# One block of value weighing moved ahead of the output projection on TensorE, in an attention and expert layer over eight batch elements

## The reference, cut to what matters

```python
h = _layernorm(x) * (1 + ca) + sa
x = x + ga * attn(h)                     # (8, 256, 128)
h = _layernorm(x) * (1 + cb) + sb
x = x + gb * experts(h)

# attn: 16 heads of 8, keys within 32 tokens of the query
Q, K, V = split(h @ W_qkv.T)
scores = where(mask, Q @ K.T / sqrt(8), -inf)
out = softmax(scores) @ V                # "the values weighed"
attn = out @ W_o.T                       # "the output projection"
```

## Time and profile before

| | us |
|---|---|
| median of three runs | 168.95 |
| their range | 168.29 to 169.29 |
| the profiled execution | 168.28 |
| its span | 166.5 |
| TensorE busy in it (matmuls) | 147.6 |
| VectorE busy | 129.4 |
| ScalarE busy | 88.6 |
| GpSimd busy | 54.9 |
| mean DMA traffic | 37 GB/s |

### The profile page before, as it was taken

How to read it: one execution, slowest core, us unless ns; L and a number is a source line. 1 busy time by engine, 2 the same in 40 slices (tenths; PEclk the granted TensorE clock), 3 DMA queues, 4 the chain that set the end, 5 groups by cost and what they waited for, 6 DMA issues and landing times.

```text
span 166.5 us, 5054 instructions
## 1 busy us (share of the span) xinstructions
PE 147.6 (89%) x1966; PEld 124.2 (75%) x1968; DVE 129.4 (78%) x353; ACT 88.6 (53%) x173; POOL 54.9 (33%) x109
## 2 busy tenths in 40 slices
PE   6799986979899989999899989998999899966943
PEld 2478875868689968997699869985998599644833
DVE  3456457698989998889899989997989888763572
ACT  3143765356838473855477456845672555535220
POOL 6422130140063605370526143523412252163030
PEclk9999999999999999999999999999999999998799
DMA  5864241102330242013401330044003400100002
GB/s 143 234 191 28 24 41 12 34 1 35 22 47 0 32 32 69 6 31 20 78 4 16 35 48 4 4 46 52 0 4 41 57 0 4 33 0 0 0 0 63
DMA packets 47430, 6.21 MB, mean 37 GB/s; under 512 B 42416, under 2 KB 47024, under 8 KB 47408
## 3 DMA queue, kind: packets, MB, share of 16 engines
q1 hardware_dynamic: 47264, 5.90, 22.6%
q10 hardware_dynamic: 144, 0.00, 0.0%
HBM read 3.81 MB, written 2.10 MB: 35 GB/s over the span
## 4 chain that ended last, share of the span: by engine, by line
PE 58%; DVE 23%; issue 9%; ACT 7%; POOL 2%; POOLq 0%; ACTq 0%; DVEq 0%
PE ps L637 8%; PE ps L669 8%; PE ps L729 7%; DVE blkmax L936 5%; PE ps L597 3%; PE ps L652 3%; PE ps L722 3%; PE ps L787 3%; PE ps L756 3%; PE ps L707 3%; DVE shift L954 2%; PE ps L709 2%; PE ps L708 2%; PE ps L611 2%; PE ps L615 2%
## 5 line engine op out<-in xcount | busy, mean ns | idle before, releaser
L352 POOL TENSOR_TENSOR act_w<-act,cw 128x512 f32<-128x512 f32 x15 | 15.7, 1044 | 49.1 <-issue 33.5
L936 DVE TRANSPOSE_TENSOR_REDUCE blkmax<-ps 128x44 f32<-128x1408 f32 x16 | 26.3, 1642 | 4.9 <-PE ps L644 4.9
L486 ACT ACTIVATE probs<-ps 128x704 f32<-128x704 f32 x32 | 23.2, 754 | 6.8 <-PE ps L652 6.0
L669 PE MATMUL ps<-probs,v_bd 128*36 128x64 f32 (+2 forms) x640 | 23.3, 227 | 0.5 <-ACT probs L486 0.5
L669 PEld LDWEIGHTS ps<-probs,v_bd 128*36 128x36 f32 x640 | 20.9, 114 | 3.0 <-issue 0.9
L637 PEld LDWEIGHTS ps<-q_sb,k_bd 32*128 32x128 f32 x640 | 19.4, 186 | 4.7 <-issue 3.4
L637 PE MATMUL ps<-q_sb,k_bd 32*128 32x96 f32 (+2 forms) x640 | 21.3, 274 | 0.6 <-ACT probs L486 0.3
L493 ACT ACTIVATE o_t<-ps 36x512 f32<-36x512 f32 x16 | 9.5, 593 | 15.8 <-PE ps L669 15.7
L499 ACT ACTIVATE tanh_g<-ps 128x512 f32<-128x512 f32 x16 | 9.6, 597 | 15.4 <-PE ps L709 15.4
L729 PE MATMUL ps<-wd_sb,act_t 128*128 128x128 f32 x128 | 16.7, 276 | 0.7 <-ACT act_t L503 0.7
L729 PEld LDWEIGHTS ps<-wd_sb,act_t 128*128 128x128 f32 x128 | 15.9, 191 | 1.0 <-ACT act_t L503 0.9
(11 more groups left out here) (102 smaller groups left out, 281.5 us busy)
## 6 DMA issues: line engine op xcount, KB each, us to landing
x_sb<-x SPq DMA_DIRECT2D x8, 128.0 KB, 2.5
v_spill<-v_sb SPq DMA_DIRECT2D x8, 128.0 KB, 2.3
v_bd<-v_spill SPq DMA_DIRECT2D x32, 32.0 KB, 2.8
out<-out_sb SPq DMA_DIRECT2D x7, 128.0 KB, 2.4
wgu_sb<-w_gu SPq DMA_DIRECT2D x1, 512.0 KB, 4.3
wm_sb<-wmod SPq DMA_DIRECT2D x1, 256.0 KB, 3.8
wd_sb<-w_down SPq DMA_DIRECT2D x1, 256.0 KB, 5.4
con<-consts SPq DMA_DIRECT2D x1, 244.0 KB, 2.9
```

Of the source, the lines that this page charges most:

```text
L352: nc.gpsimd.tensor_tensor(act_w[:, t, :].rearrange("p (e i) -> p e i", e=E), act[:, t, :].rearrange("p (e i) -> p e i", e=E), view(cw[:, t ...
L486: nc.scalar.activation(probs[:, t, hgs, cols], ps[:, hgs, cols], ACT.Exp, scale=float(DH) ** -0.5).then_inc(probs_ready, 1)
L669: last = nc.tensor.matmul(ps[p0:p0 + VW, OB, c0 + lo * KB:c0 + (hi + 1) * KB], v_bd[:, i % VB, kb, hg, :], view(probs[:, t, hg, at:at + 1] ...
L936: nc.vector.tensor_reduce(blkmax[:, t, :, live(t):live(t) + LIVE], view(ps[:, 0, live(t) * KB:live(t) * KB + 1], [[BANK, NHG], [KB, LIVE], ...
```

## The change

In the steady steps on TensorE, `weigh_values(i, 0, 0)` is issued between the transposes of the normalised attention output and the output projection, and no longer behind the second scores. Everything else stays in its place, and all waits are as they were.

```diff
                 subtract_max(i, 0, 0)
                 subtract_max(i, 0, 1)
                 transpose_on(i - 1)
+                weigh_values(i, 0, 0)
                 output_projection(i - 1)
                 up(i - 2, 1)
                 scores(i, 1)
-                weigh_values(i, 0, 0)
                 weigh_values(i, 0, 1)
                 transpose_x1(i - 1)
                 transpose_act(i - 2, 0)
```

## The result

| | before | changed |
|---|---|---|
| median of four runs | 169.01 | 182.78 |
| their range | 168.29 to 169.29 | 180.41 to 184.42 |
| profiled execution | 168.28 | 183.99 |
| its span | 166.5 | 182.2 |

The change makes the kernel slower. The ratio is 1.0708, with an interval from 1.0647 to 1.077; it is taken from those two of the four executions (181.57 and 180.41) in which TensorE's clock was held back less, and the profiled one is not among them. The same kernel, measured again later beside runs of before at 169.23, took 186.10 (185.85 to 186.30), a ratio of 1.099, from 1.0967 to 1.1014. That spread is itself part of the answer.

A forecast was written before the change was run, and what follows sets the result against it. The end was set by a lane changing between TensorE and VectorE, with the stretch hanging on the output projection's start. Profiled 168.28 + 11.4 wait - 0.3 regained = 179.4; against the median 180.05, forecast 180.0 us, range 175.5 to 185.5.

The forecast's parts named there:

- the first rival: Moved block on TensorE: values already in place, only 0.12 us lost per step, 169.6 us; chance 0.08.
- the sum: Output projection's delays in steps 2 to 7, from the values' landings plus release and block: 11.4 us in all.
- The block and the gap: Before the output projection: a 0.69 us block in a 0.47 us idle makes the projection 0.12 us late per step.
- The size of the wait: TensorE waiting for four value transfers: projection late by 2.84, 1.59, 2.05, 2.39, 1.35 and 1.15 us, 11.4 in all.
- My bounds: Output projection's total delay: 7.2 us with shortest landings and a usual spill in step 2, 16.0 with the longest.
- What comes back: Behind the projection, at the second layer norm and shifts: 0.05 us regained per step, 0.3 in all.
- The idle ahead of L597: TensorE idle ahead of the second layer norm's transposes: about 0.5 us, released by ScalarE's xn.
- The clock: TensorE's granted clock falling in the new idles: 185.1 us for three of six steps, 190.2 for all; chance 0.12.
- my own price: Cost of a granted-clock fall where TensorE is the bound: 1.7 us, read from the fall at 152 to 156.
- the two cases: Full wait at full clock, 180.0 us, chance 0.76; and the clock falling in three of six steps, 185.1 us.
- the range: Forecast time from 175.5 to 185.5 us, covering the wait's bounds and clock falls in up to three steps.
- The second rival's condition: Placed values early and TensorE's lane setting the step behind the projection: 0.57 us gained per step, 165.5 us; chance 0.04.

The follow-up runs named there:

- the idle matmuls: Four idle matmuls of 512 columns added to the changed kernel, between the transposes and the moved block: 183.06 us, ratio 1.0852.
- the two kernels with the wait alone: Order of before, with the wait for the four value transfers put ahead of the output projection: 184.59 us; with four idle matmuls ahead of that wait: 178.54 us.
- the run of the old values: Changed order with a third v_bd buffer, weighing the previous element's values in the steady steps, so no wait for its own: 170.29 us, ratio 1.0108.
- the kernel with two transfers on ScalarE: Changed kernel with the last two of the four placed-value transfers issued by ScalarE instead of SyncE in steps 3 to 7: 178.55 us, ratio 1.0539.
- one transfer on ScalarE: Changed kernel with the last of the four placed-value transfers issued by ScalarE instead of SyncE in steps 3 to 7: 179.73 us, ratio 1.0585.

## Why the prediction was right, and where it was not

- **What decides.** Right. The block's wait for its own values holds the projection. Taking the wait away left 1.6 us over the 168.74 of before on that chip (the first rival's side, though it gave 0.7), putting the wait there alone gave the projections' delays of the sum (7.5 against 7.3), and with one issue fewer on SyncE the wait shrank by 0.6 us a step.
- **The block and the gap.** The block starts 0.36 us behind L749 and takes 0.75, not 0.69; a block measured inside a pair is a little short. The move without the wait makes the projection 0.19 late and a step 0.12 to 0.15 longer (steps 3 to 6), where I had 0.12.
- **The size of the wait.** 11.0 against 11.4. The terms that rested on how long the four issues take differ both ways (step 5: 1.84 against 2.39), and the sum was 11.0 and 12.2 in the two profiles of the changed kernel and 13.9 with the idle matmuls. My bounds from 7.2 to 16.0 hold them all.
- **What comes back.** Right: 0.04 and 0.03 in the two steps that can be read so (3 and 6), where I took off 0.05. The idle ahead of L597 is 0.54, as said.
- **The clock.** Here the step failed. I held it at 1.00 in the forecast, a term put at nothing, and gave its fall a chance of 0.12; it fell in three steps of six, in both profiles of this kernel, and added 5.2 and 4.3 us in the steps. So three of the steps took 20.4 to 20.6 us where I had 18.5 to 19.7. By my own price, 180.0 + 3 x 1.7 = 185.1, the median of 182.78 lies between the two cases. That it lies in the range is in part luck: the range reached up to three falls, and the same kernel took 186.10 when it was measured again, outside it. I had taken the idle of 2.19 us without a fall as evidence against; the falls after 1.55 and 1.57 us show that one idle's length says little. The kernel of which the Trainium skill tells (TensorE: Matmul & The Clock Gate, section "HAM oscillation — how this bites in real kernels") waits some 3 to 5 us for each transfer, and every group of its matmuls starts at half clock. I had called that just this pattern, and it is not: the waits were 1.0 to 3.0 us in the changed kernel, and three of six steps were hit.
- **The second rival's condition** (TensorE's lane decides behind the projection) is refuted by the run of the old values: with the wait gone, steps 3 to 6 were 0.12 to 0.15 us longer than in before, and not 0.57 shorter.
- **Where the profile would show it.** I had said that the profile would put the idle to a transfer. It put it to the exponentials or to nothing, and only in the two kernels with the wait alone to the transfer.

## What to carry to other kernels

An instruction that moves takes all its waits with it, those too that cost nothing in its old place and are named nowhere in the profile: look up when each was met, by the landing times of the transfers, before filling a gap. A gap of 0.47 us is not worth a block of 0.75 when what stands behind it has no time to spare. And a wait on TensorE can cost twice, since the clock may fall behind it. A few idle matmuls in a wait that can't be avoided are worth a try and no more: of three tries here one won about 5 us, one won nothing, in an execution with a longer wait, and one won nothing since the fall came behind a later idle.

## What the runs showed of the hardware

- In the waits of the steps, the granted clock fell to 0.50 behind idles of 1.35, 1.55, 1.57, 1.61, 1.65, 1.94 and from 2.26 to 3.29 us, and not behind those up to 1.33 and those of 1.46 and, in the kernel with two transfers on ScalarE, 1.57; nor behind the 2.19 at the end of before. With four idle matmuls ahead of them, an idle of 2.31 us had a fall behind it (wait alone) and one of 2.33 had none (changed kernel). The fall itself came between 1.8 us before TensorE went on (step 2 with one transfer on ScalarE) and 1.3 us after it (step 4 with the wait alone).
- By the working of the table, a fall cost 1.3 to 2.2 us in the changed kernel's steps, and 1.3 to 4.1 with the wait alone.
- Four issues of 32 KB each, from one spilled tensor into 32 partitions each, took SyncE 2.67 to 3.91 us in steps 2 to 7 of all profiles, with single issues between 0.55 and 1.9 us over all steps. What makes one of them long I have not found.
- The spill of step 2 lands after 3.7 us, the others after 2.2 to 2.3, in the profile of before; its place in the changed kernel's trace is the same (issued at 39.02, the next issue at 42.75). It is not fixed: from the spill's issue to the first of the four it was 3.6 to 4.1 us in eleven profiles and 2.4 in that with two transfers on ScalarE.
